# Forming y in one operation on VectorE for the first 44 tiles of a mixture-of-experts stage

## What is computed

```python
logits = xt @ Wr + br
p = jax.nn.softmax(logits, axis=-1)
probs, idx = jax.lax.top_k(p, K)
...
h = jnp.einsum('td,edf->etf', xt, W1) + b1[:, None, :]
h = _layernorm(jax.nn.relu(h), g1, be1)
y = jnp.einsum('etf,efd->etd', h, W2) + b2[:, None, :]
y = _layernorm(jax.nn.relu(y), g2, be2)
...
out = jnp.einsum('te,etd->td', gate, y)
```

## Time and profile before

| what | value |
|---|---|
| median of 3 runs (lowest to highest) | 511.91 us (511.09 to 512.72) |
| the profiled execution, its own time | 511.78 us |
| its span, first to last instruction | 509.7 us |
| TensorE busy, share of the span | 484.1 us, 95% |
| VectorE busy | 442.7 us, 87% |
| ScalarE busy | 412.3 us, 81% |
| GpSimd busy | 359.9 us, 71% |
| mean granted TensorE clock | 0.991 |

### The profile page before, as it was taken

One profiled execution on the slowest core, in us unless ns is written; L12 is line 12 of the kernel. 1 busy time (PEld: TensorE's weight loads), 2 busy tenths in 40 slices (PEclk: granted clock), 3 DMA queues, 4 the chain that ended last, 5 costly groups with the idle time before them and its releaser, 6 DMA issues. The chain is left out here.

```text
span 509.7 us, 15082 instructions
## 1 busy us (share of the span) xinstructions
PE 484.1 (95%) x3083; PEld 371.6 (73%) x3083; DVE 442.7 (87%) x2217; ACT 412.3 (81%) x1140; POOL 359.9 (71%) x483
## 2 busy tenths in 40 slices
PE   6989999999999899999987999999999999999994
PEld 6445656555567688788876888888888888888851
DVE  6879999998888898888866899999898999999994
ACT  3679887978765788889965898998889898999884
POOL 1003666666767778888888888788788788988871
PEclk9999999999999999999997999999999999999998
DMA  6990111153111588996515877665766767667565
GB/s 165 310 246 22 49 48 44 49 131 107 60 47 50 148 175 160 183 258 176 161 47 145 199 193 178 192 199 152 214 191 147 196 209 205 173 183 208 188 178 165
DMA packets 80329, 78.36 MB, mean 154 GB/s; under 512 B 11420, under 2 KB 73015, under 8 KB 80242
## 3 DMA queue, kind: packets, MB, share of 16 engines
q1 hardware_dynamic: 71826, 60.48, 47.5%
q0 software_dynamic: 8416, 16.93, 9.3%
HBM read 55.20 MB, written 22.62 MB: 153 GB/s over the span
## 5 line engine op out<-in xcount | busy, mean ns | idle before, releaser
L683 POOL DMA_INDIRECT expert_rows<-rows_ring,slot x128 | 123.4, 964 | 94.0 <-issue 75.9
L711 POOL DMA_INDIRECT expert_results<-y,target x119 | 120.7, 1014 | 30.1 <-issue 24.1
L1649 PE MATMUL bank<-W,h2T 128*128 x720 | 96.4, 277 | 2.3 <-DVE wmod L1419 1.4
L1649 PEld LDWEIGHTS bank<-W,h2T 128*128 128x128 f32 x720 | 87.6, 191 | 12.9 <-issue 6.2
L914 ACT ACTIVATE v<-wmod 128x128 f32<-128x128 f32 x135 | 41.8, 310 | 43.1 <-DVE vg L1430 38.8
L1631 PE MATMUL bank<-W1hi,h3hi 128*128 x135 | 65.7, 487 | 1.3 <-DVE h3lo L1184 1.3
L792 ACT ACTIVATE n<-X,nm,rs 128x128 f32<-128x128 f32 x128 | 54.1, 485 | 13.5 <-DVE nm L1363 12.8
L1419 DVE SCALAR_TENSOR_TENSOR wmod<-bank,rse,shifts 128x128 f32<-128x128 f32 x119 | 41.0, 345 | 26.7 <-PE bank L1649 18.1
L1189 DVE BATCH_NORM_STATS2 stf<-h1T 128x6 f32<-128x512 f32 x90 | 59.3, 660 | 0.0
L1639 PE MATMUL bank<-ident_wr,h1T 128*128 128x128 f32 x360 | 54.7, 275 | 0.0
L807 ACT ACTIVATE h2T<-bank 128x512 f32<-128x512 f32 x90 | 52.9, 588 | 1.3 <-PE bank L1639 1.3
(11 more groups left out here) (249 smaller groups left out, 1192.2 us busy)
## 6 DMA issues: line engine op xcount, KB each, us to landing
shifts<-expert_shifts SPq DMA_DIRECT2D x119, 192.0 KB, 3.7
hrow<-expert_rows SPq DMA_DIRECT2D x135, 65.0 KB
xi<-expert_results SPq DMA_DIRECT2D x12, 512.0 KB, 5.5
out_x<-X SPq DMA_DIRECT2D x15, 256.0 KB
X<-in_L_attn_x SPq DMA_DIRECT2D x7, 512.0 KB, 7.4
b_ring<-b_two_parts SPq DMA_DIRECT2D x135, 4.0 KB
W1lo<-in_L_ffn_W SPq DMA_DIRECT2D x4, 512.0 KB, 6.7
expert_rows<-rows_ring,slot POOLq DMA_INDIRECT x128
```

Source lines behind the costliest of these rows:

```text
L683: nc.gpsimd.indirect_dma_start(out=rows_d, out_offset=bass.IndirectOffsetOnAxis(ap=slot[q][:, n // TOPK, n % TOPK:n % TOPK + 1], axis=0), ...
L711: nc.gpsimd.indirect_dma_start(out=results_d, out_offset=bass.IndirectOffsetOnAxis(ap=target[i % TARGETS][:], axis=0), in_=y[k], in_offset ...
L1649: ins = mm(acc, rT[i % DEPTH][:, ch * P:(ch + 1) * P], W2[:, bass.ds(e * CF + ch, 1), :], start=(ch == 0), stop=(ch == CF - 1))
```

## The change

For tiles 0 to 43 (`ROWS_UNTIL`), as for the last five before, VectorE forms y in one operation, `direct_y`, right behind vg. ScalarE's scaling and GpSimd's addition are left out for them. For tiles 44 to 129 all stays as it was. The semaphores are counted apart, one for tiles of either kind. What releases a slot of constants (`load_shifts`) is then `direct_y_ready` for tiles 0 to 43. In the file of the changed kernel all lines behind the insertion stand some lines lower.

```diff
+        ROWS_UNTIL = 44
+
+        def direct(i):
+            return i >= LAST_SHIFTED or i < ROWS_UNTIL
...
             def load_shifts(i):
-                if last_user(i) is not None:
-                    sp.wait_ge(y_ready, last_user(i) + 1)
+                user = last_user(i)
+                if user is not None and direct(user):
+                    sp.wait_ge(direct_y_ready, direct_count(user))
+                elif user is not None:
+                    sp.wait_ge(y_ready, shifted_count(user))
...
-                add_shift(i)
+                if not direct(i):
+                    add_shift(i)
...
-                if on(s - 8, LAST_SHIFTED):
+                if on(s - 8, EXPERT_TILES) and not direct(s - 8):
                     act.wait_ge(vg_ready, s - 7)
                     act.wait_ge(rse_ready, s - 4)
                     if on(s - 8 - VS, EXPERT_TILES):
-                        act.wait_ge(y_ready, s - 7 - VS)
+                        act.wait_ge(y_ready, shifted_count(s - 8 - VS))
                     nc.scalar.activation(vs[(s - 8) % VS], vg[q][:], ACT.Copy, scale=rse[q][:, 1:2]).then_inc(vs_ready, 1)
...
-            def last_y(i, p):
+            def direct_y(i, p):
                 k = ring(i)
                 dve.wait_ge(vg_ready, i + 1)
                 dve.wait_ge(rse_ready, i + 4)
-                dve.wait_ge(results_stored[last_user(i) % RESULTS], result_count(last_user(i)))
+                if last_user(i) is not None:
+                    dve.wait_ge(results_stored[last_user(i) % RESULTS], result_count(last_user(i)))
                 vec.scalar_tensor_tensor(wide(y[k]), wide(vg[p][:]), rse[p][:, 1:2], wide(shift_rows[k][:, 2 * D:3 * D]),
-                                         ALU.mult, ALU.add).then_inc(last_y_ready, 1)
+                                         ALU.mult, ALU.add).then_inc(direct_y_ready, 1)
...
-                if s - 7 >= LAST_SHIFTED:
-                    last_y(s - 7, p)
+                if direct(s - 7):
+                    direct_y(s - 7, p)
```

More of the change, by code:

```diff
@@ L243, in adaln_ssm_moe_kernel, with direct_count, shifted_count @@
         EARLY_H = 4
+        ROWS_UNTIL = 44
+        def direct(i):
+            return i >= LAST_SHIFTED or i < ROWS_UNTIL
+        def direct_count(i):
+            return sum(direct(n) for n in range(i + 1))
+        def shifted_count(i):
+            return i + 1 - direct_count(i)
         def tiles_for(b):
@@ L385, in adaln_ssm_moe_kernel @@
         out_stored = sem("out_stored")
-        lead_ready, half_gate_ready, gates_ready, last_y_ready = sem("lead_ready"), sem("half_gate_ready"), sem("gates_ready"), sem("last_y_ready")
+        lead_ready, half_gate_ready, gates_ready, direct_y_ready = sem("lead_ready"), sem("half_gate_ready"), sem("gates_ready"), sem("direct_y_ready")
         early_loaded = [sem(f"early_loaded{q}") for q in range(2)]
@@ L695, in add_shift @@
                 k = ring(i)
-                pool.wait_ge(vs_ready, i + 1)
+                pool.wait_ge(vs_ready, shifted_count(i))
                 if last_user(i) is not None:
@@ L705, in store_results @@
                     pool.wait_ge(results_stored[i % RESULTS], result_count(i - RESULTS))
-                if i >= LAST_SHIFTED:
-                    pool.wait_ge(last_y_ready, i + 1 - LAST_SHIFTED)
+                if direct(i):
+                    pool.wait_ge(direct_y_ready, direct_count(i))
                 else:
-                    pool.wait_ge(y_ready, i + 1)
+                    pool.wait_ge(y_ready, shifted_count(i))
                 pool.nop(nofuse=True)
@@ L766, in _ @@
                         early_out_of(b, j)
-                add_shift(i)
+                if not direct(i):
+                    add_shift(i)
                 if i > 0:
                     store_results(i - 1)
-                if i % 2 == 1 and sent[0] < B * J * TOPK:
+                if i % 2 == 1 and i < ROWS_UNTIL:
                     store_next(1)
@@ L1424, in reciprocals @@
                 dve.wait_ge(sde_ready, s - 3)
-                if on(s - 9, LAST_SHIFTED):
-                    dve.wait_ge(vs_ready, s - 8)
+                if on(s - 9, EXPERT_TILES) and not direct(s - 9):
+                    dve.wait_ge(vs_ready, shifted_count(s - 9))
                 vec.reciprocal(rse[p][:, both], sde[p][:, both]).then_inc(rse_ready, 1)
```

## The result

The changed kernel takes 508.98 us in the median of 20 runs (507.42 to 510.96), the kernel before 512.54 us beside it (20 runs, 510.36 to 514.16). The ratio is **0.9924, with a 95% interval of 0.9913 to 0.9936**. The sign and the range of the prediction held; the size did not. The gain is 0.8% and not 1.4%: 3.6 us of the 7.3 forecast. The prediction's own mark of a wrong forecast, the tiles not about 7 us earlier by tile 54, is met as well: they are 3.2 us earlier there.

A forecast was written before the change was run, and what follows sets the result against it. The prediction took TensorE's pace of 2.30 us a tile as the bound, broken by one 8.2 us pause from a late load of constants. Its terms: 511.8 - 8.2 + 0.6 + 0.3 = 504.5 us, range 502.5 to 510.

The forecast's parts named there:

- the pause: Tile 47's rows, queued behind tile 40's late constants, stall TensorE and its clock slows; removing this saves 8.2 us.
- table stretch: Steps 7 to 15, where VectorE also writes the second table: the added y's delay TensorE by 1.2 us.
- the wait in step 23: VectorE's 1.26 us wait for constants shrinks if VectorE arrives later, so only 0.3 us of 1.2 is paid.
- nine groups: Groups of four tiles, steps 16 to 51: VectorE's work exceeds TensorE's pace by 0.07 us each, 0.6 us in all.
- The stores: GpSimd's result stores free y's buffers in time, with 9 us of room at tile 40.
- y's own price: The added operation directly behind vg costs VectorE 0.38 us a tile, 16.7 us over 44 tiles.
- rival (c): GpSimd's store issue holds y by 0.24 us in all 44 tiles: slower, 516 us; chance 0.09 together with another rival.
- VectorE's cushion: VectorE's idle time before v0 falls from 26.7 to under 15 us; its busy share rises by about 15 us.
- 9.27 against 9.20: VectorE's serial work in four steps with y, against TensorE's time for four tiles, in us: the two become equal.
- rival (a): VectorE becomes the bound by more than counted, 0.46 us a tile: 508 us; chance 0.19 together with another rival.
- The bounds: y's price lies between 0.26 us a tile, overlapped and hidden (503.6 us), and 0.24 more a tile from a 0.57 us operation.

The follow-up runs named there:

- e3: The changed kernel with VectorE forming y for tiles 32 to 43 only, tiles 0 to 31 as before the change: 509.32 us, ratio to before 0.9924.
- e4: The kernel before, plus one unread operation of y's form on VectorE behind vg in the first 44 tiles: 513.52 us, ratio to before 1.0001.
- e6: The changed kernel with y moved to the end of VectorE's step, behind the last statistics: 504.12 us, ratio to before 0.9840.
- e1: The changed kernel with y moved one operation later in VectorE's step, behind h3lo: 504.93 us, ratio to before 0.9838.
- e5: The changed kernel with TensorE reading the next expert number ahead of the relu's wait in every fourth step up to 51: 506.31 us, ratio to before 0.9898.
- e8: The changed kernel with y at the end of VectorE's step and formed by VectorE for all 135 tiles: 512.61 us, ratio to before 1.0000.
- e7: The changed kernel with both y behind h3lo and the expert number read ahead of the relu's wait: 505.56 us, ratio to before 0.9862.

## Why the pause went as forecast and the gain was half as large

By its own steps, with the profiled executions (511.8 and 508.3 us):

| Term | forecast | measured |
|---|---|---|
| pause removed (tiles 46 to 54) | -8.2 | -8.2 |
| table stretch, to tile 18 | +1.2 | +1.6 |
| taken up by the wait in step 23 | -0.9 | -0.9 |
| nine groups, tiles 18 to 54 | +0.6 | +4.3 |
| behind tile 54 | 0 | -0.3 |
| sum | -7.3 | -3.5 |

How the measured column is read: nine undisturbed groups are 82.8 us; the kernel before took 91.92 from tile 18 to 54, of which 8.19 are the pause and 0.93 the wait in step 23; the changed kernel took 87.07, 4.27 more than 82.8. Of these, 3.8 are nine times the 0.42 us of the groups from tile 26 to 46; the other 0.5 lies in the first two and the last two groups, which are a little longer.

**The pause: right**, in place, cause and size. SyncE's wait is gone, no transpose waits, the clock is 1.00 in the window of the earlier trace rows, and e3 shows the wait gone with 12 tiles alone. Tile 40's load went out 3.6 us later than I said, since VectorE itself was 3.6 us later, and it was still early enough.

**The stores: right.** The wait view of the changed kernel has no wait of VectorE for `expert_results`; e3 shows what it looks like when they are late. GpSimd's store of tile 42 starts at 280.62 (I had 279 for the last of the 44); tile 43's stands behind the first addition, which starts at 287.25 after 4.39 us of waiting for ScalarE. I had 282 for it, so that was 5 us off, but nobody waited for it.

**y's own price: right**, 0.38 a tile. In the first 44 tiles vg takes 333 and y 352 ns on average, as the groups by line of the changed kernel, 195 to 285 us, show. Compare.

```profile
L1426 DVE SCALAR_TENSOR_TENSOR y<-vg,rse,shifts 128x128 f32<-128x128 f32 x21 | 7.4, 352 | 0.7
L1445 DVE SCALAR_TENSOR_TENSOR vg<-v,mve,shifts 128x128 f32<-128x128 f32 x21 | 7.0, 333 | 0.0
```

That rules out rival (c): GpSimd issues stores throughout, and y isn't held; the longest takes 0.41 us. The Trainium skill (SBUF — State Buffer, section "SBUF: two separate sides") has the rule by which (c) could have come, if a store counted as GpSimd's read of SBUF; the 352 ns speak against that reading, as the prediction took it. With GpSimd's additions it is otherwise: in the same stretch of the kernel before, vg takes 377 ns on average with single ones of 0.67, and e4's extra operation 422. So leaving the additions out also made vg some 0.03 to 0.04 us shorter, a gain that the sum doesn't have. The 0.57 that the prediction calls the longest vg isn't the longest of its trace either (0.67 at 283.91 us), but the forecast doesn't hang on it.

**VectorE's cushion: right in kind.** Its busy time rose by 12.9 us (442.7 to 455.6; I had 15), and the idle time ahead of v0 fell from 26.7 to 12.2, by the costliest groups of the changed kernel's page, which answer.

```profile
L1434 DVE SCALAR_TENSOR_TENSOR wmod<-bank,rse,shifts 128x128 f32<-128x128 f32 x119 | 40.9, 344 | 12.2 <-PE bank L1664 10.7
```

**The table stretch: 1.6 for 1.2**, and the step-23 wait took up what I said. That was a fair term. With y last (e6) the stretch from 10 to 18 costs 0.7 in place of 1.6; I haven't separated which of its operations pays.

**The step that failed** is "9.27 against 9.20, 9 x 0.07 = 0.6 us". It was a comparison of two sums of durations, and it held both to be independent. First, 9.27 was 9.37, for 0.03 in each of three plain steps, a small thing, but with no cushion each hundredth is paid in full: 9 x 0.10 = 0.9 us. Second, and larger, the comparison allowed for one link alone from VectorE to TensorE, v0, to which I gave 0.7 us of room. There is a second one, by way of ScalarE: y stands ahead of the statistics that end VectorE's step, so these came later against the rest, and with them the square root, the relu behind it in ScalarE's order, and TensorE's issue. Its room was 0.68 us by the rows of before shown above, and I didn't look for it. The room goes with the cost: 0.09 us of room and 0.38 of "issue" in the changed kernel, 0.34 and 0.19 in e1, 0.69 and none in e6. I had even said of ScalarE that the square root would come earlier, since ScalarE is relieved of 44 scalings. The opposite came about: in a plain step the square root started 0.28 us ahead of v0 (231.91 and 232.19 us in the kernel before) and now starts 0.04 ahead (235.05 and 235.09). ScalarE now stands in front of it for 29.1 us, in 44 waits, as the waits of the changed kernel say; the idle time by itself costs nothing (e1 still has 22.6 us of it).

```profile
ACT sde L940 <- DVE mve L1458: 29.1, 44, 0.7
```

An engine that is given less work isn't earlier with what it receives from another. The two halves, 0.17 (9.37 against 9.20) and 0.25, together are the 0.42 us a group from tile 26 to 46, 2.1 us there; e5 gives one half back, e6 both, and e1 nearly both (0.25 us is left).

So rival (a) is what happened, and my prices for it (0.46 a tile in place of 0.38) came near the time (508), by the wrong reason: y costs 0.38, and it is its place in the order that costs the rest.

**The bounds.** I gave 503.6 us as the time if y overlapped the next operation and cost 0.26. e1 and e6 are that case: 504.9 and 504.1, as ratios 0.9838 and 0.9840, and 503.6 is 0.984 of the 511.9 that I started from. The lower end was a matter of one line of code, which I treated as an unknown of the hardware.

## What to carry to other kernels

When an operation is added to an engine that is nearly as busy as the bound, don't compare the sums of a round alone: go through every operation behind the new one in that engine's round, ask who waits for it, and follow each of these waits on to the bound engine with its room in us. Then don't put the new operation directly behind the operation whose result it reads; here one place further back was the difference between 0.8% and 1.6%. To put it behind the last of those for which someone waits gave the awaited relu its whole room back (e6), but no time beyond e1 that the runs could tell. And before a pause is taken out, look at what it hides: costs ahead of it are nearly free as long as it stands.

## What the runs showed of the hardware

- On VectorE an operation that reads the result of the one directly ahead of it, behind a semaphore, starts 0.37 us after it; with another operation between, each starts 0.20 to 0.26 after the one ahead (e1's rows). I knew both numbers from the rows of before, but not that moving one operation would change the one for the other without any other loss.
- A read of an expert number by TensorE's sequencer costs nothing as long as it can run ahead of the engine (0.09 us ahead of the product's weight load in the kernel before and in e6). Standing behind a wait that is met only just in time, it shows as 0.38 to 0.57 us of "issue" in front of the next weight load (the changed kernel); moved ahead of that wait it leaves 0.10 to 0.12 in most steps, 0.20 in the one shown (e5).
- In the stage where GpSimd also adds for the early output, y takes 389 ns on average in e8, single ones up to 0.51 us, against 352 in the first 44 tiles of the changed kernel.
- Beside GpSimd's additions of y, VectorE's operations on two tensors in SBUF get longer, beside its issue of scatters they don't: e4's extra operation takes 422 ns on average and up to 0.66 us, the changed kernel's y 352 ns and at most 0.41, both from 195 to 285 us.
- The granted clock fell to 0.50 to 0.60 at 172 to 174 us in three of ten profiles (e3, e7, e8), which made the group of four tiles there about 1 us longer. By tile 26 the difference was gone, because a wait for constants, 30 to 40 us later, was shorter by it.
